# Register loads of a graph kernel's edge count: 32-bit places spread over partitions, or 16-bit places in one row; segment tables stored at once or in seven parts

## The chip, the cores and the metric

The kernel runs on one core of one Trainium2 chip. The metric is the time on the device in microseconds, the median of several executions. One further execution is recorded by the hardware profiler; all rows below come from it.

## What is computed

Four graph layers stand behind each other, each with a layer norm, a ReLU and a residual sum around it, over 3125 nodes of 128 features and one list of 103125 edges, sorted by destination.

```python
edge_index = jnp.stack([src, dst])
h = jnp.maximum(_layernorm(x, axis=-1), 0.0)
x = x + _L0_gnn_ref(h, edge_index, ...)      # segment_sum(x[src], dst) @ W_rel + b + x @ W_root, batch norm, relu
h = jnp.maximum(_layernorm(x, axis=-1), 0.0)
x = x + _L1_gnn_ref(h, ..., src, dst)        # two layers: mean over neighbours
h = jnp.maximum(_layernorm(x, axis=-1), 0.0)
x = x + _L2_gnn_ref(h, edge_index, ...)      # attention over edges, 8 heads
h = jnp.maximum(_layernorm(x, axis=-1), 0.0)
x = x + _L3_gnn_ref(h, ..., edge_index, edge_type_8)   # two layers, a weight matrix for each of 8 edge types
```

The first two layers need sums over neighbours only, so the kernel counts the edges between each pair of nodes once, in a table `adj` in DRAM, and multiplies by it.

## The kernel before, in words

**The stage of the change** builds `adj`. The edges lie in 806 tiles of 128. They are gone through in 84 epochs of 19 steps (`EPOCHS`, `STEPS_OF`). A step is one product on TensorE: a one-hot of the edges' source digit (128 columns) times a one-hot of 100 cells (`CELLS`), added into PSUM at a place that depends on the data. So each step has a place, a number up to 7600, that TensorE's instruction queue has to have in a register before it can issue the product. A twentieth place of each epoch (`SLOTS` is 20) says where the last block of the epoch before lies, which is carried over from SBUF by the product at L784.

The places are worked out on VectorE at lines 450 to 460 into `steprow`, a tile of 84 partitions (one for each epoch) with 32-bit integers; the last of these instructions gives the mark `stepped`. `places_of(e, lo, hi)` (L750) loads the places `lo` to `hi` of epoch `e` into TensorE's registers with one load instruction, from partition `e`. Four epochs are a window (`GROUP`), and `count_edges` spreads the loads over it: at the end of a window's fourth epoch it loads 20, 20 and the first 8 (`FEW`) places of the next three epochs; in the middle of the third epoch, before its step 8, the other 12; at that epoch's end the 20 of the fourth.

The other engines run beside this, each in a loop of its own. VectorE builds the one-hots of each epoch in two instructions (`compare_epochs`, L416 and L419), two epochs ahead at most, and in some epochs the moments of a tile of `X`. ScalarE (`move_out`, L809) copies each epoch's PSUM half into one of two windows in SBUF (`adj_window`, `chunk_and_window`), and from epoch 54 on does a tile of the first layer norm in each epoch; before that it waits for `s_seg`. SyncE's queue (`store_windows`, L831) stores a window of 3850 KB to `adj` when its four epochs are out, one store after the other; ScalarE may write a window again when its store has landed.

**The segment tables** (`relf`, `twice`, `seg`: for each tile of 128 edges where segments begin and end) are made on GpSimd at lines 716 to 727 and stored to `rel_tile` and `seg_tile` behind the fourth window's store (`w == 3`, L832 to L837). The attention layer reads them back some 1000 us later. They lie where ScalarE writes from epoch 54 on, hence its wait.

**The start.** SyncE's queue issues the inputs' transfers up to L376, then goes on to the windows' stores. `s_joint`, a trip of the step blocks through DRAM (L354 to L358), has the form of the trip that the change adds.

Of the kernel before, what the change touches and what calls it, by code (L numbers as in the profile page):

```python
# [4 lines left out]

F32 = mybir.dt.float32
I32 = mybir.dt.int32
F16 = mybir.dt.float16
B16 = mybir.dt.bfloat16
ALU = mybir.AluOpType  # L10
# [36 lines left out]
KT = 7  # L47
# [4 lines left out]
STEPS = EPOCHS * STEPS_OF  # L52
QUARTER = STEPS // 4
GROUP = 4
FEW = 8
WINDOWS = EPOCHS // GROUP
SPANNED = GROUP * STEPS_OF + 1
# [1 line left out]
CHUNKS = 7  # L59
DST = CHUNK * WD  # L60
BLOCKS = CHUNK * CHUNKS
assert (WINDOWS - 1) * GROUP * STEPS_OF - (ET - 1) >= CHUNK and RELU_FROM + NT <= EPOCHS
assert EPOCHS % GROUP == 0 and STEPS % 4 == 0 and STEPS >= ET + BLOCKS - 1 and KT * P >= BLOCKS
BEGUN = ((0, 4), (0, KT), (0, KT), (0, KT))
HELD = ((0, 4), (0, KT), (0, KT), (3, KT))
# [52 lines left out]
def build(nc, a, out):  # L118
    with ExitStack() as ctx:
# [69 lines left out]
        def dram(name, shape, dt=F32):  # L189
            return nc.dram_tensor(name, shape, dt, kind="Internal").ap()  # L190
# [2 lines left out]
        xs_t, xd_t = dram("xs_t", [NP, RW]), dram("xd_t", [W, RW])  # L193
        rel_t = [dram(f"rel_table{j}", [R * NP, P]) for j in (0, 1)]
        rel_tile = dram("rel_tile", [KT * P, P], F16)
        step_row = dram("step_row", [1, STEPS + 1 + EPOCHS], F16)
        seg_tile = dram("seg_tile", [KT * P, SEG])
        piece_t = dram("piece_t", [HEADS, PT * P // 2, 4])
# [21 lines left out]
        cells = tmp(dense, "edge_cell", [P, EPOCHS, SLOTS], F16)  # L220
        iota_lo = tmp(dense, "iota_lo", [P, P, STEPS_OF], F16)
        iota_cell = tmp(dense, "iota_cell", [P, CELLS, 2], F16)
        steprow = tmp(dense, "steprow", [EPOCHS, 32], I32)
        dstf = invdeg[:, 4 * P:(4 + KT) * P].rearrange("p (k e) -> p k e", e=P)
        relf = invdeg[:, (4 + KT) * P:(4 + 2 * KT) * P].bitcast(F16)[:, 0:KT * P].rearrange("p (k e) -> p k e", e=P)
        twice = invdeg[:, (4 + 2 * KT) * P:(4 + 3 * KT) * P].rearrange("p (k e) -> p k e", e=P)
        seg = H[:, :, :].rearrange("p t d -> p (t d)")[:, 0:KT * 3 * P].rearrange("p (k a e) -> p k a e", k=KT, a=3)
        epochrow = tmp(dense, "epochrow", [1, WINDOWS, 16], I32)
        windowrow = tmp(dense, "windowrow", [1, WINDOWS], I32)
        early = ExitStack()  # L230
# [194 lines left out]
        for j in range(4):  # L425
            T.need(found[j], centred)
            if j > 1:
                T.need(lod[j - 2], spread[j - 2])
            placed_d.append(look(4 + j, j, 1, 0))
            T.need(both, bsd[j])  # L430
            placed_c.append(look(j, j, 2, 1))
            T.need(within)
            if j > 1:
                T.need(celled[j - 2])
            looked = look((6, 7, 4, 5)[j], j, 0)
            A.need(placed_d[j])
            spread.append(A.did(nc.scalar.activation(far[:, quarter(j)], pb[4 + j][:, 0:QUARTER], ACT.Square,
                                                     bias=centre[:, 0:1])))
            A.need(looked)
            lod.append(A.did(nc.scalar.activation(los[:, 21 * j:21 * j + 21, :].rearrange("p e k -> p (e k)"),  # L440
                                                  pb[(6, 7, 4, 5)[j]][:, 0:QUARTER], ACT.Copy)))
            celled.append(cells_of_quarter(j))
            if j == 0:
                V.after(lod[0])
                compare_epoch(0)
            if j == 1:
                A.did(nc.scalar.activation(dstf[:, :, :], drow[:, :, :], ACT.Copy))
                copied = A.did(nc.scalar.activation(twice, twice.bitcast(I32), ACT.Copy))
                V.need(s_joint.now())
                V.did(nc.vector.tensor_scalar(jr[:, :], joint[:, 0:STEPS_OF], joint[:, 0:1], None, ALU.subtract))  # L450
                V.did(nc.vector.tensor_scalar(steprow[:, STEPS_OF:SLOTS], joint[:, 0:1], joint[:, STEPS_OF:SLOTS],
                                              float(CELLS), ALU.subtract, ALU.mult))
                V.did(V.after().tensor_scalar(turns[:, :], jr[:, :], float(SLOTS // 4), None, ALU.is_ge))
                for q in (2, 3):
                    V.did(V.after().scalar_tensor_tensor(out=turns[:, :], in0=jr[:, :], scalar=float(q * SLOTS // 4),
                                                         in1=turns[:, :], op0=ALU.is_ge, op1=ALU.add))
                V.did(V.after().tensor_scalar(jr[:, :], jr[:, :], float(CELLS), None, ALU.mult))
                stepped = V.did(V.after().scalar_tensor_tensor(
                    out=steprow[:, 0:STEPS_OF], in0=turns[:, :], scalar=float(512 - SLOTS // 4 * CELLS), in1=jr[:, :],
                    op0=ALU.mult, op1=ALU.add))  # L460
                b0w = b0[:, :].rearrange("p (w g) -> p w g", g=GROUP)
                V.did(nc.vector.tensor_scalar(b0[:, :], steps_of[:, :, 0], -1.0, float(CELLS), ALU.add, ALU.mult))
                V.did(V.after().tensor_copy(windowrow[:, :], b0w[:, :, 0]))
                windowed = V.did(V.after().tensor_tensor(epochrow[0:1, :, 0:GROUP], b0w,
                                                         b0w[:, :, 0:1].to_broadcast([1, WINDOWS, GROUP]), ALU.subtract))
        T.need(idn, s_raw.now(), lod[2])
        for j, n in enumerate(raw):
            tw = T.did(nc.tensor.transpose(pb[4][:, j * P:(j + 1) * P], wraw[n], ident[:, :]))
# [279 lines left out]
                    first_norm["shift"] = rows_shift(0, NT, (root_n, 1))  # L748

        def places_of(e, lo, hi):  # L750
            place = nc.values_load_multi_w_load_instructions(
                steprow[e:e + 1, lo:hi], engines=(ENG.PE,), min_val=0, max_val=(SPANNED - 1) * CELLS,
                skip_runtime_bounds_check_because="made on the chip from counts")[1]
            return [nc.s_assert_within(v, 0, 2048 - CELLS, skip_runtime_bounds_check_because="made on the chip")
                    for v in place[:STEPS_OF - lo]] + list(place[STEPS_OF - lo:])

        def count_edges():
            T.need(stepped)
            place = {0: places_of(0, 0, SLOTS)}
            T.need(celled[3], A.now())  # L760
            for e in range(EPOCHS):
                half = sums[:, (e % 2) * 2048:(e % 2 + 1) * 2048]
                if e > 1:
                    nc.tensor.wait_ge(eout_n, e - 1)
                for j in range(4):
                    nc.tensor.matmul(half[:, j * 512:j * 512 + SLOTS // 4 * CELLS], zeros[:, 0:P],  # L766
                                     zeros[:, 0:SLOTS // 4 * CELLS], start=True, stop=False)
                nc.tensor.wait_ge(ehot_n, e + 1)
                places = place.pop(e)
                for k in range(STEPS_OF):  # L770
                    if e % GROUP == 2 and k == FEW:
                        places = places + places_of(e, FEW, SLOTS)
                    m = nc.tensor.matmul(half[:, bass.ds(places[k], CELLS)], hot_lo[e % 2][:, :, k], hot_cell[e % 2][:, k // 2, :, k % 2],  # L773
                                         start=False, stop=False)
                m.then_inc(estep_n, 1)
                for j in range(1 if e else 0, 4):
                    m = nc.tensor.matmul(half[:, j * 512:j * 512 + 1], zeros[:, 0:P], zeros[:, 0:1], start=False, stop=True)
                if e == 0:
                    place.update({1: places_of(1, 0, SLOTS), 2: places_of(2, 0, FEW)})
                if e % GROUP == 2:  # L780
                    place[e + 1] = places_of(e + 1, 0, SLOTS)
                if e:
                    nc.tensor.wait_ge(eout_n, e)
                    m = nc.tensor.matmul(half[:, 0:CELLS], ident[:, :],  # L784
                                     filled[(e - 1) // GROUP % 2][:, bass.ds(places[STEPS_OF], CELLS)],
                                     start=False, stop=True)
                m.then_inc(ebuilt_n, 1)
                if e + 1 < EPOCHS and e % GROUP == GROUP - 1:
                    place.update((n, places_of(n, 0, SLOTS)) for n in (e + 1, e + 2))
                    place[e + 3] = places_of(e + 3, 0, FEW)  # L790
# [29 lines left out]
        def store_windows():  # L820
            nc.sync.wait_ge(*windowed)
            for w in range(WINDOWS):
# [8 lines left out]
                nc.sync.dma_start(adj[:, bass.ds(first, SPANNED * CELLS)], filled[w % 2][:, :]).then_inc(s_adj, 16)  # L831
                if w == 3:  # L832
                    nc.sync.wait_ge(*relled)
                    s_seg.did(nc.sync.dma_start(rel_tile.rearrange("(k p) e -> p k e", p=P), relf))
                    s_seg.did(nc.sync.dma_start(seg_tile[:, 3 * P:SEG].rearrange("(k p) s -> p k s", p=P), twice))
                    s_seg.did(nc.sync.dma_start(seg_tile[:, 0:3 * P].rearrange("(k p) s -> p k s", p=P),
                                                seg[:, :, :, :].rearrange("p k a e -> p k (a e)")))  # L837

        def load_chunk(c, b, *marks):
            for mark in marks:  # L840
# [960 lines left out]
```

## Time and profile before

| | |
|---|---|
| runs of the kernel | 4201.55, 4203.5, 4205.0 us; median 4203.5 |
| the profiled execution's own time | 4200.0 us |
| its span, first to last instruction | 4198.7 us |
| busy over the span | TensorE 72%, GpSimd 56%, VectorE 45%, ScalarE 17% |
| TensorE's mean granted clock | 0.702 of full speed |

The span is what the rows below count in, from 0; the time on the device is 1.3 us more. Busy shares are means over stages with different limits: the stage of the change lies in the first tenth of the span.

In the rows, PE is TensorE, PEld its weight loads, DVE VectorE, ACT ScalarE, POOL GpSimd, SP SyncE; a q behind the name is the engine's instruction queue. "x19" is a count. In brackets stands the idle time before, and what ended it; "issue" says that nothing in the profile did.

### The profile page before, as it was taken

The numbers are of one execution on the slowest core, as the hardware profiler recorded it, in microseconds if no ns is written. First come the engines' busy times: TensorE is split into PE (matmuls) and PEld (weight loads), VectorE is DVE, ScalarE is ACT, GpSimd is POOL, SyncE is SP. The second block draws the span as 40 slices with busy tenths as digits, with TensorE's granted clock in tenths as the row PEclk, the third lists the DMA queues.
The fourth block names the chain that finished last, engine by engine and source line by source line (L and its number), as shares of the span: only waits on it lengthen the run. The fifth ranks groups of instructions, "written<-read, shape, count | busy, mean of one in ns | idle before, by whom it ended". The sixth has DMA issues, their size and how long they took to land.

```text
span 4198.7 us, 42410 instructions
## 1 busy us (share of the span) xinstructions
PE 3033.3 (72%) x12147; PEld 1985.2 (47%) x12147; DVE 1903.7 (45%) x4160; ACT 713.2 (17%) x1945; POOL 2354.3 (56%) x2464
## 2 busy tenths in 40 slices
PE   6677889997888888887476666666677666666666
PEld 4555445554656656665243333333344333334334
DVE  6555675558889889897621111111122111111112
ACT  4344010002434434344300000000010000000000
POOL 3000000006777777775257777777775777777776
PEclk8777899998999989898665555555566555555555
DMA  4554745545444454553132222212233221211222
GB/s 178 209 217 199 321 192 225 216 167 132 118 112 116 114 111 119 111 119 83 42 126 53 53 52 53 53 52 53 53 100 112 53 53 52 53 53 53 53 53 64
DMA packets 237155, 456.14 MB, mean 109 GB/s; under 512 B 64259, under 2 KB 184001, under 8 KB 231816
## 3 DMA queue, kind: packets, MB, share of 16 engines
q1 hardware_dynamic: 159144, 291.46, 19.5%
q0 software_dynamic: 77792, 161.98, 15.6%
q8 instruction: 112, 1.84, 0.2%
q14 instruction: 107, 0.88, 0.1%
HBM read 336.69 MB, written 116.52 MB: 108 GB/s over the span
## 4 chain that ended last, share of the span: by engine, by line
PE 30%; DMA 27%; POOL 23%; issue 14%; DVE 4%; ACT 1%; SPq 0%; ACTq 0%; DVEq 0%; POOLq 0%
DMA edge_buffers<-rel_table,relidx 25%; POOL round_buffers L1209 15%; PE sums L872 9%; PE sums L661 8%; POOL edge_buffers L633 8%; PE sums L773 3%; PE sums L766 3%; PE sums L1699 2%; PE sums L784 1%; DMA adj<-adj_window 0%; DVE logits L1408 0%; PE sums L1253 0%; DMA adj_chunk<-adj 0%; DVE positive L1405 0%; PE sums L1331 0%
## 5 line engine op out<-in xcount | busy, mean ns | idle before, releaser
L633 POOL DMA_INDIRECT edge_buffers<-rel_table,relidx x1612 | 1529.5, 949 | 584.6 <-PE sums L661 415.1
L661 PE MATMUL sums<-edge_buffers 128*128 128x128 f32 x3224 | 1250.2, 494 | 748.7 <-DMA edge_buffers<-rel_table,relidx 744.8
L661 PEld LDWEIGHTS sums<-edge_buffers 128*128 128x128 f32 x3224 | 799.3, 309 | 1202.6 <-issue 1201.8
L1209 POOL DMA_INDIRECT round_buffers<-xs_t,srcs x806 | 763.7, 948 | 571.5 <-DMA xd_t<-round_buffers 326.1
L644 DVE TENSOR_SCALAR edge_buffers<-iota,rel 128x128 f32<-128x128 f32 x1612 | 334.4, 298 | 1639.2 <-PE sums L661 1639.2
L690 ACT ACTIVATE trio<-sums,c_L_b 128x256 f32<-128x256 f32 (+1 forms) x16 | 8.0, 500 | 2014.1 <-PE sums L665 2014.1
L1022 POOL IOTA trio<- 128x806 int32 x1 | 0.8, 805 | 566.1 <-ACT H L576 566.1
L1253 PE MATMUL sums<-round_buffers,ident 128*128 128x408 f32 x620 | 278.5, 533 | 25.8 <-DMA round_buffers<-xs_t,srcs 22.2
L1256 PEld LDWEIGHTS sums<-round_buffers 128*128 128x128 f32 x1612 | 244.1, 198 | 75.9 <-issue 65.2
L1353 ACT ACTIVATE trio<-sums 128x128 f32 x806 | 223.8, 278 | 279.1 <-PE sums L1331 205.5
L1331 PE MATMUL sums<-round_buffers 128*128 128x128 f32 x1612 | 243.0, 301 | 4.0 <-issue 2.0
L1256 PE MATMUL sums<-round_buffers 128*128 128x136 f32 x1612 | 245.6, 286 | 0.0
L872 PE MATMUL sums<-chunk_and_window,H 128*128 128x448 f32 x600 | 231.5, 546 | 7.3 <-issue 6.1
L1331 PEld LDWEIGHTS sums<-round_buffers 128*128 128x128 f32 x1612 | 218.5, 211 | 17.5 <-issue 14.4
L416 DVE TENSOR_TENSOR trio<-iota_lo,edge_lo 128x2432 f16<-128x2432 f16 x84 | 125.9, 1498 | 169.7 <-PE sums L773 168.8
L1405 DVE TENSOR_TENSOR positive<-positive,sums 128x384 f32<-128x384 f32 x310 | 152.9, 493 | 75.8 <-ACT positive L1343 75.5
L773 PEld LDWEIGHTS sums<-trio 128*128 128x128 f16 x1596 | 142.6, 152 | 75.5 <-issue 66.2
L773 PE MATMUL sums<-trio 128*128 128x100 f16 x1596 | 147.1, 257 | 42.7 <-issue 42.6
L872 PE MATMUL sums<-adj_chunk,H 128*128 128x448 f32 x450 | 173.6, 546 | 3.5 <-DMA adj_chunk<-adj 3.5
L872 PEld LDWEIGHTS sums<-chunk_and_window,H 128*128 128x128 f32 x600 | 115.2, 193 | 119.4 <-issue 117.7
L1394 DVE TENSOR_SCALAR round_buffers<-sums,pair_column 128x416 f32<-128x416 f32 x248 | 159.7, 644 | 12.0 <-PE sums L1271 11.2
L1408 DVE TENSOR_REDUCE logits<-positive 128x24 f32<-128x384 f32 x310 | 155.3, 501 | 10.7
(326 smaller groups left out, 2871.0 us busy)
## 6 DMA issues: line engine op xcount, KB each, us to landing
chunk_and_window<-adj SPq DMA_DIRECT2D x10, 5600.0 KB, 16.2
round_buffers<-xd_t SPq DMA_DIRECT2D x806, 68.0 KB
adj_chunk<-adj SPq DMA_DIRECT2D x9, 5600.0 KB, 16.0
adj<-adj_window SPq DMA_DIRECT2D x11, 3850.0 KB, 12.4
adj<-chunk_and_window SPq DMA_DIRECT2D x10, 3850.0 KB, 12.5
edge_buffers<-rel_table,relidx POOLq DMA_INDIRECT x1612, 2.5
rel_table<-table_stages SPq DMA_DIRECT2D x50, 512.0 KB, 2.6
round_buffers<-xs_t,srcs POOLq DMA_INDIRECT x806
```

The costliest lines, as they stand in the source:

```text
L633: nc.gpsimd.indirect_dma_start(slot(t), None, table[:, :], bass.IndirectOffsetOnAxis(ap=index[:, t:t + 1], axis=0)).then_inc(slot_sem(t), 16)
L644: made = nc.vector.tensor_scalar(round_hots(i)[:, k, :], iota[:, :], rel[:, t:t + 1], None, ALU.is_equal)
L661: nc.tensor.matmul(sums[:, bass.ds(place[k], P)], slot(t), round_hots(i)[:, k, :], start=False, stop=False).then_inc(summed_n, 1)
L773: m = nc.tensor.matmul(half[:, bass.ds(places[k], CELLS)], hot_lo[e % 2][:, :, k], hot_cell[e % 2][:, k // 2, :, k % 2], start=False, stop ...
L872: m = nc.tensor.matmul(ps.rearrange("p (b w) -> p b w", w=WD), tables[:, hi, :], held[b][:, :, hi, :], start=(hi == 0), stop=(hi == HI - 1))
L1209: nc.gpsimd.indirect_dma_start(rows[r % RING][:, k * RW:(k + 1) * RW], None, xs_t[:, :], bass.IndirectOffsetOnAxis(ap=srcs[:, t:t + 1], ax ...
L1253: nc.tensor.matmul(pb[2 + q % 2][:, 0:(hi - lo) * RW], ident[:, :], rows[r % RING][:, lo * RW:hi * RW], start=True, stop=False)
L1256: m = nc.tensor.matmul(pb[2 + q % 2][:, (k - lo) * RW:(k - lo + 1) * RW], hotT[r % 2][:, k * P:(k + 1) * P], win[r % 2][:, k * RW:(k + 1) ...
L1331: m = nc.tensor.matmul(pb[6 + q % 2][:, (k - lo) * P:(k - lo + 1) * P], msg[:, k * P:(k + 1) * P], hot[r % 2][:, k * P:(k + 1) * P], start ...
L1353: nc.scalar.activation(pairs[:, bass.ds(at[k], P)], pb[6 + q % 2][:, (k - lo) * P:(k - lo + 1) * P], ACT.Copy).then_inc(out_n, 1)
L1394: nc.vector.tensor_scalar(hotT[r % 2][:, j * QUART:(j + 1) * QUART], spread, paircol[:, 0:1], None, ALU.is_equal).then_inc(hotT_n, 1)
L1408: nc.vector.tensor_reduce(lgs[:, :].rearrange("p (h k) -> p k h", k=U)[:, lo:hi, :], lv.rearrange("p (k h c) -> p k h c", h=HEADS, c=HD), ...
```

## The change

The places are worked out as before, but written as 16-bit integers (`steprow` is now a 16-bit view of a tile of 32-bit words, 16 in each of 84 partitions). Two new transfers take the ten words of each epoch through DRAM (`reg_row`) into one row on partition 0, `regrow`, with 12 words for each epoch. Epoch 0 is still loaded from `steprow`; all others are loaded from `regrow`, as 16-bit numbers, after a wait for the second transfer (`T.need(regged)`, behind epoch 0's steps). How many registers a load fills, and when, is the same.

The three stores of the segment tables behind window 3 become three stores, of a seventh each, behind each of the windows 3 to 9.

```diff
+I16 = mybir.dt.int16
+WORDS = 12
...
+        reg_row = dram("reg_row", [EPOCHS, WORDS], I32)
...
-        steprow = tmp(dense, "steprow", [EPOCHS, 32], I32)
+        stepwords = tmp(dense, "step_words", [EPOCHS, 16], I32)
+        steprow = stepwords[:, :].bitcast(I16)
...
+        regrow = tmp(dense, "regrow", [1, EPOCHS * WORDS], I32)
...
+        s_regs = Dma(sem("s_register_row"))
+        nc.sync.wait_ge(*stepped)
+        regged = s_regs.did(nc.sync.dma_start(reg_row[:, 0:SLOTS // 2], stepwords[:, 0:SLOTS // 2]))
+        nc.sync.wait_ge(*regged)
+        regged = s_regs.did(nc.sync.dma_start(
+            regrow[:, :].rearrange("a (e k) -> a e k", k=WORDS)[:, :, 0:SLOTS // 2],
+            reg_row.rearrange("(a e) k -> a e k", a=1)[:, :, 0:SLOTS // 2]))
...
         def places_of(e, lo, hi):
+            row = regrow[:, :].bitcast(I16)[0:1, 2 * e * WORDS + lo:2 * e * WORDS + hi] if e else steprow[0:1, lo:hi]
             place = nc.values_load_multi_w_load_instructions(
-                steprow[e:e + 1, lo:hi], engines=(ENG.PE,), min_val=0, max_val=(SPANNED - 1) * CELLS,
+                row, engines=(ENG.PE,), min_val=0, max_val=(SPANNED - 1) * CELLS,
...
                 if e == 0:
+                    T.need(regged)
                     place.update({1: places_of(1, 0, SLOTS), 2: places_of(2, 0, FEW)})
...
                 if w == 3:
                     nc.sync.wait_ge(*relled)
-                    s_seg.did(nc.sync.dma_start(rel_tile.rearrange("(k p) e -> p k e", p=P), relf))
-                    s_seg.did(nc.sync.dma_start(seg_tile[:, 3 * P:SEG].rearrange("(k p) s -> p k s", p=P), twice))
-                    s_seg.did(nc.sync.dma_start(seg_tile[:, 0:3 * P].rearrange("(k p) s -> p k s", p=P),
-                                                seg[:, :, :, :].rearrange("p k a e -> p k (a e)")))
+                if 3 <= w < 3 + KT:
+                    rows = slice((w - 3) * P, (w - 2) * P)
+                    s_seg.did(nc.sync.dma_start(rel_tile[rows, :], relf[:, w - 3, :]))
+                    s_seg.did(nc.sync.dma_start(seg_tile[rows, 3 * P:SEG], twice[:, w - 3, :]))
+                    s_seg.did(nc.sync.dma_start(seg_tile[rows, 0:3 * P], seg[:, w - 3, :, :].rearrange("p a e -> p (a e)")))
```

## Rows read from the trace of the kernel before

**Rows 1.** Busy time by stretch: us, engines, TensorE clock, DMA share, GB/s
```profile
35.00:440.00 405.00, 287.12 (x2353) 216.17 (x2354) 225.16 (x200) 165.85 (x115) 33.59 (x12) 0.75 0.51 212
```

**Rows 2.** The chain that ended last, 35 to 440 us, by line
```profile
by line: PE sums L773 32.5%; PE sums L766 26.6%; issue 24.3%; PE sums L784 10.6%; DMA adj<-adj_window 4.9%; ACT adj_window L809 3.6%; PE sums L777 1.2%; ACT chunk_and_window L809 0.9%; ACTq L795 0.1%; ACTq L809 0.1%; ACT w_L_n L471 0.0%; AC
```

**Rows 3.** Timeline of TensorE, 384.5 to 402.5 us: start, us, what
```profile
393.13 1.48 PE L773 MATMUL sums<-trio 128*128 128x100 f16 x11 [2.16 <-issue]
...
402.19 0.58 PE L766 MATMUL sums<-zeros 128*128 128x500 f16 x2 [2.14 <-ACT adj_window L809]
```

**Rows 4.** Register loads of L751, one each: duration in ns, start in us
```profile
L751 PEldq TENSOR_LOAD <-steprow x1: 594/594/594, 39.6 to 39.6; - x1
...
L751 PEldq TENSOR_LOAD <-steprow x1: 849/849/849, 43.8 to 43.8; - x1
...
L751 PEldq TENSOR_LOAD <-steprow x1: 3464/3464/3464, 117.8 to 117.8; - x1
...
L751 PEldq TENSOR_LOAD <-steprow x1: 6004/6004/6004, 122.7 to 122.7; - x1
...
L751 PEldq TENSOR_LOAD <-steprow x1: 2647/2647/2647, 390.3 to 390.3; - x1
...
L751 PEldq TENSOR_LOAD <-steprow x1: 1379/1379/1379, 394.4 to 394.4; - x1
```

**Rows 5.** Timeline of SyncE's queue, 50 to 445 us
```profile
53.96 0.36 SPq L831 DMA_DIRECT2D adj<-adj_window  x1
...
111.65 0.33 SPq L831 DMA_DIRECT2D adj<-chunk_and_window  x1
...
113.69 8.77 SPq L836 DMA_DIRECT2D seg_tile<-H  x1
...
135.58 0.37 SPq L831 DMA_DIRECT2D adj<-adj_window  x1
...
384.38 0.33 SPq L831 DMA_DIRECT2D adj<-chunk_and_window  x1
...
402.16 0.33 SPq L831 DMA_DIRECT2D adj<-adj_window  x1
...
421.01 0.33 SPq L831 DMA_DIRECT2D adj<-chunk_and_window  x1
...
439.88 0.33 SPq L831 DMA_DIRECT2D adj<-adj_window  x1
```

**Rows 6.** Loads of 1, 4, 13, 3 and 8 registers at other lines: min/median/max ns
```profile
L823 SPq TENSOR_LOAD <-windowrow x21: 262/271/951, 34.4 to 421.4; - x21
...
L795 ACTq TENSOR_LOAD <-epochrow x21: 307/310/507, 34.8 to 419.0; - x21
...
L649 PEldq TENSOR_LOAD <-offrow x124: 1091/1102/2026, 2128.9 to 4174.1; - x124
...
L1599 PEldq TENSOR_LOAD <-pair_place x1: 964/964/964, 2010.2 to 2010.2; - x1
...
L1599 PEldq TENSOR_LOAD <-pair_place x1: 1942/1942/1942, 2024.8 to 2024.8; - x1
```

**Rows 7.** DMA busy in tenths, 40 slices of 384 to 404 us
```profile
DMA  0090910909091590919010100000001000000590
```

**Rows 8.** Groups of VectorE in that window: busy us, mean ns
```profile
L416 DVE TENSOR_TENSOR trio<-iota_lo,edge_lo 128x2432 f16<-128x2432 f16 x4 | 6.0, 1493 | 7.7 <-PE sums L773 7.6
...
L419 DVE TENSOR_TENSOR trio<-iota_cell,edge_cell 128x2000 f16<-128x2000 f16 x4 | 4.8, 1192 | 0.0
```

**Rows 9.** DMA issues, 20 to 45 us: KB each, us to landing
```profile
piece_dst<-in_piece_col SPq DMA_DIRECT2D x1, 6.5 KB, 8.1
```

**Rows 10.** Waits of SyncE's queue, 20 to 60 us
```profile
SPq L356 <- DMA step_row<-step_block: 0.9, 1, 0.9
```

**Rows 11.** Busy time by window of the stretch, columns as rows 1
```profile
384.40:402.20 17.80, 12.25 (x113) 9.61 (x111) 10.28 (x8) 8.89 (x9) 0.00 (x0) 0.90 0.53 223
402.20:421.00 18.80, 13.94 (x113) 10.57 (x114) 10.54 (x9) 8.68 (x8) 0.00 (x0) 0.70 0.49 211
```

More of the change, by code:

```diff
@@ L61 @@
 BLOCKS = CHUNK * CHUNKS
-assert (WINDOWS - 1) * GROUP * STEPS_OF - (ET - 1) >= CHUNK and RELU_FROM + NT <= EPOCHS
+assert (WINDOWS - 1) * GROUP * STEPS_OF - (ET - 1) >= CHUNK and GROUP * (4 + KT) <= RELU_FROM and RELU_FROM + NT <= EPOCHS
 assert EPOCHS % GROUP == 0 and STEPS % 4 == 0 and STEPS >= ET + BLOCKS - 1 and KT * P >= BLOCKS
```

## The prediction

> **What bounds the kernel now.** I first cut the span into stretches. The count of edges is the stretch from 35 to 440 us [rows 1]: 405 us, no engine over 75% busy, TensorE's mean granted clock 0.75, the DMA engines half used. So no engine's work is the bound as it stands. The chain of that stretch [rows 2] gives 24.3% to "issue", that is to TensorE waiting for nothing that the profile shows, no line of VectorE's among the first ten, and a few per cent to ScalarE. The timeline of TensorE in one window says where this lies [rows 3]: it stands idle 2.16 us before the last 11 steps of the window's third epoch and 2.14 us before the next window.
>
> The register loads of L751 fill just these holes [rows 4] (105 in all: one for each of 84 epochs, and a second in 21 of them). The one at 390.3 us takes 2.65 us and ends at 392.98; the steps go on at 393.13. A load stops TensorE's instruction queue. The reader is to see that the queue is the bound: from one store of a window to the next, 384.38 to 402.16, are 17.78 us [rows 5]; the loads in it are one of 12 registers (2.65), three of 20 (about 1.38 each) and one of 8 (about 0.60), 7.4 us in all, and 10.4 us are left for the instructions of four epochs, 2.6 us each. Over the stretch a window takes (439.88 - 53.96) / 20 = 19.3 us.
>
> What sets a load's price? A load that nothing disturbs costs 0.27 us for 1 register and 0.31 for 4 [rows 6], 0.59 for 8, 0.85 for 12, 1.38 for 20 [rows 4]; one of 13 takes 1.10 [rows 6]. So it is one read of 0.26 us for each four registers, 16 bytes, and one more for the thirteenth. Three registers cost 0.96, near three reads, and 8 that begin off a 16-byte boundary (place 3 of their row) cost 1.94, 0.24 for each register [rows 6]: what isn't a whole aligned piece seems to be read one by one.
>
> And what disturbs one: the same 12 registers cost 0.85 us at 43.8, before any store, and 2.65 at 390.3 or, the longest, 3.46 at 117.8 while a window is being stored [rows 4]. The DMA engines start eight rounds of packets from 385.0 to 393.0 us, 1.15 us apart, so they are full until some 394.3 [rows 7] (a slice shows packets where they begin). The load at 390.3 lies in that, the one at 394.4 just behind it. I take 2.8 us for the twenty such loads, nearer to the undisturbed window's, so a read takes about 0.93 us beside a store. The load of 20 at 122.7 lies in the segment tables' transfer and takes 6.00 us, and that window takes 135.58 - 111.65 = 23.9 us [rows 4, 5].
>
> **The change, part by part.**
>
> *Loads of 16-bit places.* The trace has no load of 16-bit numbers, so the price has to be bounded. Below: if a read brings 16 bytes whatever the type, 8 places come in one, and rows of 12 words (48 bytes) keep each epoch, and place 8 of it, aligned: 20 places (40 bytes) are 3 reads instead of 5, 12 are 2 instead of 3, 8 are 1 instead of 2. Above: every place by itself, as in the load off the boundary (0.24 us each), 4.9 us for 20. I take the lower, because every load on aligned data in this trace, on three engines, goes by 16 bytes; the row of 3 registers is what speaks against it.
>
> Per window then: the 12 go from 2.8 to 2 x 0.93 = 1.87 (-0.93). The next load, of 20, used to start 10.0 us after the store's issue (394.4 - 384.4), as the store's packets ran out. It now starts at +9.1, and one or two of its 3 reads meet the store: 0.93 + 0.27 + 0.27 = 1.5 to 0.93 + 0.93 + 0.27 = 2.1, where it cost 1.38; I take +0.3. The three behind the fourth epoch go from 1.38 + 1.38 + 0.60 to 0.85 + 0.85 + 0.31, -1.35. Sum -2.0 us; without the collision -2.8. Over 20 windows -40 us.
>
> Is something else late next? VectorE's comparison needs 1.49 + 1.19 = 2.7 us an epoch [rows 8], 10.7 in a window, plus 0.3 in the epochs with moments; a window of 17.3 us covers it. The store's 10 to 12 us fit too, though stores wait for each other. Neither binds.
>
> The Trainium skill, page "Runtime: NRT & Kernel Launch", section "Instruction fetch mechanics", gives a register load (it speaks of loads from HBM) about 200 ns for each register, in bulk too. By that 20 registers would cost 4.0 us; the trace has 1.38 [rows 4], 70 ns each, so the trace disagrees on the size. But the rule counts registers, not bytes, and by it a narrower type would save nothing in any load, and the sum would be the detour's 6 us alone.
>
> *The row's way through DRAM.* SyncE's queue issues two transfers that weren't there, with a wait between them, and TensorE waits for the second (`regged`) before it loads epoch 1. The wait for `stepped` is over when SyncE comes to it, behind the issue at 33.66. The transfer at 33.66 lands 8.1 us later, at 41.8 [rows 9], behind the index tables that are issued before it. The first new one is issued at about 34.4 and lands behind it, at 42; the second is issued then and takes 1 us (a like one, 3 KB, was waited for 0.9 us [rows 10]) to 3 us. So `regged` stands at 43.5 to 45.5, where TensorE was through with its loads at 40.2 (39.6 + 0.6 [rows 4]), the 1.4 us load of 20 before that one included. It now ends them at about 44.5 + 0.85 + 0.31 = 45.7: +5.5 us, once. Nothing hides it, as ScalarE and VectorE wait for TensorE's epoch 1. Behind it on SyncE stands only the first window's store, at 54. If the transfers overtook the queue it would be near 0; I keep 0 to +8.
>
> *Segment tables in seven parts.* Now three transfers (224 + 448 + 1344 KB) follow the fourth store, SyncE is held 8.77 us by the last [rows 5], and the 20-register load meets them. In parts, about 1 us of DMA stands behind each of seven stores. The load of 6.00 us falls back to about 1.5 (-4.5); in seven windows one read more of the load at +9.1 falls into the transfer, 0.65 us each (+4.5). I cost it at nothing, -5 to +5. ScalarE's wait for the tables at epoch 54 comes at about 36 + 54 x 4.8 = 295 us; the last part goes out behind the tenth store, by 36 + 10 x 19.3 = 229 us at the latest.
>
> **Sum.** -40 + 5.5 + 0 = -34.5 us. The profiled execution took 4200.0 (span 4198.7), so 4165.5; it lies 3.5 below the median of the runs shown, 4203.5, and on that scale I predict **4169 us**.
>
> **The rivals.** 0.2%, 8.4 us, is about what a measurement of this kernel can tell from no change.
>
> 1. *As above*, 4169, own range 4140 to 4190. Chance 0.54.
> 2. *A load costs by registers*, four to a read of whatever width. For it: all loads here are of 32-bit numbers, so the trace can't tell 16 bytes from four registers. Against it: 8 registers off a 16-byte boundary cost 1.94 [rows 6], so the address counts. The loads stay, the row's detour stays: +6, with the tables 0, so 4209. It is also the case in which the change does nothing for the loads. Chance 0.16. (The rule of the Trainium skill cited above, from "Runtime: NRT & Kernel Launch", points to this case.)
> 3. *The rest behind whole pieces is read singly.* 20 places are two pieces and four single ones, 6 reads; 12 are 5; 8 are 1. For it: 13 registers, and 3. The 12 beside the store: four reads of 0.93 and one free, 4.0 (+1.2); the 20 each 1.6 (+0.24, three times); 8 at 0.31 (-0.3). +1.6 a window, +32, with the detour +38: 4242. Chance 0.12.
> 4. *16-bit places are read one by one*, the other side of the bound. 12: five in the store and seven after, 6.3 us (+3.5); 20: 4.9 (+3.5, three times); 8: 1.9 (+1.3). +15.3 a window, 306 in all, 4203.5 + 306 + 6 = 4515. The forecast turns from gain to loss where 20 places cost more than about 1.3 us. Chance 0.10.
> 5. *More than forecast*: the load of 20 escapes the store (-2.8 a window, -57) and TensorE's clock falls less, since its idle times get shorter. The window from 402.2 had a mean of 0.70 of the clock and took 18.85 us (421.01 - 402.16), the one before it 0.90 and 17.78 [rows 5, 11]: 1 us a window, -20 at most. Against it: the stretch's mean is 0.75 [rows 1], and the idle times get shorter, but don't end. With the detour: -72, 4132. Chance 0.08.
>
> **The numbers.** Faster 0.54 + 0.08 = 0.62, same 0.16, slower 0.22. The range has to reach over rivals 2 and 3 and most of 5: 4130 to 4250; rival 4 lies outside.
>
> **What would show it.** The 20-register loads at about 0.85 us and those of 8 at 0.31 (rival 2: 1.38 and 0.60; 3: 1.6 and 0.31; 4: 4.9 and 1.9); the 12 beside a store near 1.9; the 20 loaded at the end of a window's third epoch longer than the others by 0.5 or more; stores of windows 17.3 us apart; epoch 1's loads beginning at 43 to 46 us; no load of 6 us, and no window of 24. The prediction is wrong first of all if the read isn't 16 bytes, then if something I called covered, a comparison or a store, takes up the holes that the loads leave.

## The result, and the profile after

The change made the kernel slower: 4577.01 us, the median of 4 runs (4568.01 to 4579.06), against 4204.25 (4201.55 to 4205.31) for the kernel before on the same chip. The ratio is 1.0882, with an interval of [1.0867, 1.0897]; that is +372.8 us. The forecast was -34.5. Ratios here leave out an execution that lies far above the others of its kernel; there was one, of 7972 us, among the ten of few12_seven below.

Where is the time? First the page's part 2 of the kernel after, its span in 40 slices of 114 us each:

```profile
span 4566.7 us, 42430 instructions
...
PE   4333333989978888888866666666667666666666
...
PEclk7666665989989999999987555555557555555555
```

The first seven slices, some 800 us, are a stage in which TensorE is busy a third of the time. Next the timeline of SyncE's queue, the stores of the first window, of two in the middle and of the last:

```profile
69.03 0.37 SPq L845 DMA_DIRECT2D adj<-adj_window  x1
...
445.83 0.34 SPq L845 DMA_DIRECT2D adj<-adj_window  x1
482.64 0.34 SPq L845 DMA_DIRECT2D adj<-chunk_and_window  x1
...
818.26 0.33 SPq L845 DMA_DIRECT2D adj<-adj_window  x1
```

A window takes (818.26 - 69.03) / 20 = 37.46 us, where it took 19.3 [rows 5]. The last store is issued 378.4 us later than before (439.88 [rows 5]); behind it the kernel is 10 us shorter than it was (4566.7 - 818.3 against 4198.7 - 439.9). So the whole loss lies in the count of edges. The chain from 35 to 820 us and the same window by itself:

```profile
by line: issue 56.6%; PE sums L786 16.6%; PE sums L779 14.5%; PE sums L798 5.5%; ACT adj_window L823 2.6%; ACT chunk_and_window L823 2.4%; DMA adj<-adj_window 1.4%; DMA reg_row<-step_words 0.9%; PE sums L790 0.6%; DMA regrow<-reg_row 0.3%; 
```
```profile
445.83:482.64 36.81, 14.22 (x112) 10.23 (x112) 10.64 (x10) 8.86 (x6) 0.00 (x0) 0.64 0.25 108
```

"issue" was 24.3% [rows 2]. The work in a window is what it was: 14.22 us of matmuls where two windows before had 12.25 and 13.94 [rows 11]. In the window's timeline of TensorE (start, us, what, and the idle time before it) the holes stand out:

```profile
460.01 1.82 PE L779 MATMUL sums<-zeros 128*128 128x500 f16 x4 [16.29 <-issue]
...
470.32 1.48 PE L786 MATMUL sums<-trio 128*128 128x100 f16 x11 [1.73 <-issue]
...
476.44 0.74 PE L798 MATMUL sums<-chunk_and_window,ident 128*128 x2 [4.58 <-issue]
```

The register loads, L764 in this kernel, one each, in ns, the last field the start in us; they answer to [rows 4]:

```profile
L764 PEldq TENSOR_LOAD <-regrow x1: 11262/11262/11262, 446.7 to 446.7; - x1
...
L764 PEldq TENSOR_LOAD <-regrow x1: 1916/1916/1916, 458.0 to 458.0; - x1
...
L764 PEldq TENSOR_LOAD <-regrow x1: 2852/2852/2852, 467.3 to 467.3; - x1
...
L764 PEldq TENSOR_LOAD <-regrow x1: 4720/4720/4720, 471.6 to 471.6; - x1
...
L764 PEldq TENSOR_LOAD <-regrow x1: 6031/6031/6031, 479.3 to 479.3; - x1
```

Undisturbed, 20 places now cost 4.72 us, 12 cost 2.85, 8 cost 1.92: each place 0.24 us, with no step at four or at eight. 20 places cost 1.38 before, and the same 12 cost 0.85 undisturbed. Where a load lies makes it worse. The window's store is issued at 445.83; the strip of the DMA engines (tenths, 40 slices of 440 to 500 us, 1.5 us each) shows it from 446 to 455 us, and the load of 20 at 446.7 lies in it and takes 11.26:

```profile
DMA  0000779779000000000000000000297797700000
```

Before, the load in the store was one of 12 registers and the three long ones lay outside. Now the first of the three loads at a window's end (at 479.3, behind the fourth epoch) takes 6.03 us, the store is issued meanwhile, the second load of 20 meets it, and the load of 12 at 467.3, 21 us behind the store's issue, is free of it.

All 105 loads together take 533.3 us in this trace and 163.9 in the one before, a difference of 369.4. That is nearly all of the 378.4 us by which the last store is later.

### The profile page after: what moved, and what is told of

The parts are those of the page before. It is cut to its first block, busy times and chain, and to the rows that moved or that the text cites. A ratio compares the mean times of both kernels' runs of the same rounds, so it can differ in the third digit from the quotient of the medians.

```text
span 4566.7 us, 42430 instructions
## 1 busy us (share of the span) xinstructions
PE 3038.7 (67%) x12147; PEld 1985.7 (43%) x12147; DVE 1902.3 (42%) x4160; ACT 712.9 (16%) x1945; POOL 2353.2 (52%) x2464
## 4 chain that ended last, share of the span: by engine, by line
PE 28%; DMA 24%; issue 20%; POOL 19%; DVE 7%; ACT 2%; SPq 0%; ACTq 0%; DVEq 0%; POOLq 0%
DMA edge_buffers<-rel_table,relidx 23%; POOL round_buffers L1224 11%; PE sums L887 8%; POOL edge_buffers L645 8%; PE sums L673 7%; PE sums L786 3%; PE sums L779 2%; PE sums L1714 2%; PE sums L798 1%; DVE logits L1423 1%; DVE positive L1420 1%; DVE round_buffers L1429 1%; DVE round_buffers L1409 1%; DVE round_buffers L1451 1%; PE sums L1268 1%
## 5 line engine op out<-in xcount | busy, mean ns | idle before, releaser
L779 PE MATMUL sums<-zeros 128*128 128x500 f16 x336 | 125.9, 516 | 346.9 <-issue 346.9
L779 PEld LDWEIGHTS sums<-zeros 128*128 128x128 f16 x336 | 42.2, 131 | 385.6 <-issue 377.7
L1409 DVE TENSOR_SCALAR round_buffers<-sums,pair_column 128x416 f32<-128x416 f32 x248 | 159.8, 644 | 11.2 <-PE sums L1286 9.9
```

Source lines behind the costliest of these rows:

```text
L1409: nc.vector.tensor_scalar(hotT[r % 2][:, j * QUART:(j + 1) * QUART], spread, paircol[:, 0:1], None, ALU.is_equal).then_inc(hotT_n, 1)
```

## The experiments

Ten kernels ran, in three groups, each on one chip beside the kernel before. On the chip of the first four the kernel before took 5164.9 us, on that of the last two 5062.7, on that of the other four 4203.4; what is longer on the first two lies behind the stage of the change, so ratios are taken on the same chip, and lengths of the stage are compared with [rows 5].

### The row alone, with 32-bit words (row32)

```diff
-WORDS = 12
+WORDS = 20
-        steprow = stepwords[:, :].bitcast(I16)
+        steprow = stepwords[:, :]
...
-            row = regrow[:, :].bitcast(I16)[0:1, 2 * e * WORDS + lo:2 * e * WORDS + hi] if e else steprow[0:1, lo:hi]
+            row = regrow[0:1, e * WORDS + lo:e * WORDS + hi] if e else steprow[0:1, lo:hi]
```

It is the kernel after, trip through DRAM and seven parts included, but with places of 32 bits.

> The changed kernel with everything kept (trip through DRAM, one row on partition 0, tables in seven parts) but the places as 32-bit words, 20 words for each epoch. Theory, the type does it: loads cost 1.38, 0.85 and 0.59 us again and only the later start of epoch 1 is left, 4204 + 6 = 4210 us. Rival, the row does it (a load from a row on partition 0 that a DMA wrote, or the wait): loads of 4.7 us remain, 4560 to 4580.

Measured: ratio 0.9991 [0.9976, 1.0006]. The loss is gone. Its register loads, of epochs 1 and 2, and of a window's 12 and 20:

```profile
L764 PEldq TENSOR_LOAD <-regrow x1: 1377/1377/1377, 44.1 to 44.1; - x1
...
L764 PEldq TENSOR_LOAD <-regrow x1: 596/596/596, 45.5 to 45.5; - x1
...
L764 PEldq TENSOR_LOAD <-regrow x1: 2644/2644/2644, 366.1 to 366.1; - x1
...
L764 PEldq TENSOR_LOAD <-regrow x1: 1359/1359/1359, 370.2 to 370.2; - x1
```

The prices are those of [rows 4]. So neither the row on partition 0 nor the trip costs anything in a load. The trip delays the first window's store by 4.9 us (58.89 against 53.96 [rows 5]), or by 6.2 against the kernel `seven` below, where it is issued at 52.70.

The ratio is under the forecast's 1.0014 all the same, and the traces point to a reason: from the row the loads are shorter. In the kernel before, an undisturbed load of 8 takes 0.587 us from partition 34 and 0.614 from partition 30, and the load of 12 beside a store takes 3.15 to 3.46 us from partitions 18 to 26 and 50 to 62, and 2.52 to 2.92 from the others. From partition 0, in row32, the same two take 0.586 to 0.596 and 2.34 to 2.99. Here is the load of 12 of epoch 50, before and in row32:

```profile
L751 PEldq TENSOR_LOAD <-steprow x1: 3324/3324/3324, 275.2 to 275.2; - x1
...
L764 PEldq TENSOR_LOAD <-regrow x1: 2637/2637/2637, 273.2 to 273.2; - x1
```

The loads of a window are 0.37 us shorter than in `seven`, some 7 us in all, about what the trip costs; the last store is issued at 435.21 here and at 435.80 there.

### 16 bits alone, without the row (part16)

```diff
-        steprow = tmp(dense, "steprow", [EPOCHS, 32], I32)
+        stepwords = tmp(dense, "step_words", [EPOCHS, 16], I32)
+        steprow = stepwords[:, :].bitcast(I16)
```

It is the kernel before with this edit only.

> The kernel before with 16-bit places, each epoch still in a partition of its own, loaded from there: no row, no trip, no wait, tables stored at once. Theory, the type does it: every place is a read of its own, 4.7 us for 20 where no store runs, 4577 less the later start (8 us), 4560 to 4575. Rival, the row: loads as before, 4200 to 4210.

Measured: ratio 1.0741 [1.0704, 1.0778], +385.6 us. All of its loads in one row (min/median/max), and one of 20 that lies in the segment tables' transfer, the table store at once being in this kernel:

```profile
L753 PEldq TENSOR_LOAD <-step_words x105: 1916/4739/16968, 31.9 to 815.2; - x105
...
L753 PEldq TENSOR_LOAD <-step_words x1: 16968/16968/16968, 179.8 to 179.8; - x1
```

The type alone brings the loss. It is 15 us more than the forecast's upper end. A window takes 38.06 us, where the kernel after needs 37.46: the load beside the table stores takes 17.0 us, 12.2 there, and an undisturbed one of 20 takes 4.72 to 4.99 us with the partition, always 4.72 there.

### The segment tables alone (seven)

```diff
-                if w == 3:
+                if 3 <= w < 3 + KT:
```

It is the kernel before with the stores in seven parts, as the change has them.

> The kernel before with the segment tables stored in seven parts alone. Both theories: no load of 6 us and no window of 24 us any more (-4.5), something back in seven windows; 4195 to 4207. If the parts were what costs, hundreds of us.

Measured: ratio 0.9986 [0.9971, 1.0002], 5157.54 us against 5164.9. The longest load of 20 takes 2.00 us, and the longest of all 3.43:

```profile
L751 PEldq TENSOR_LOAD <-steprow x105: 588/1390/3432, 31.9 to 427.9; - x105
```

The last store is issued at 435.80, 4.1 us earlier than [rows 5]; 1.3 of these it has at the first store already, before the edit acts. The interval takes in no change; the trace points to a gain of some 3 us, the medians to one of 7.

### 32 bits off the 16-byte boundary (shift32)

```diff
-        steprow = tmp(dense, "steprow", [EPOCHS, 32], I32)
+        steprow = tmp(dense, "steprow", [EPOCHS, 32], I32)[:, 1:32]
```

> The kernel before with the 32-bit places moved by one word in each partition, so that no load begins on a 16-byte boundary; nothing else. Theory, 32-bit words come four at a time only from a 16-byte boundary and singly otherwise, 0.24 us each as 16-bit places do: 4.8 us for 20, 4560 to 4580. Rival, the boundary has no part in it and what the later line (L1599) showed was disturbance: 4204.

Measured: ratio 1.0708 [1.0681, 1.0734], +366.7 us. Loads of 12, 20, 20, 20 and 8 registers in one window:

```profile
L751 PEldq TENSOR_LOAD <-steprow x1: 2869/2869/2869, 359.2 to 359.2; - x1
...
L751 PEldq TENSOR_LOAD <-steprow x1: 4732/4732/4732, 363.4 to 363.4; - x1
...
L751 PEldq TENSOR_LOAD <-steprow x1: 6039/6039/6039, 371.2 to 371.2; - x1
...
L751 PEldq TENSOR_LOAD <-steprow x1: 9913/9913/9913, 377.3 to 377.3; - x1
...
L751 PEldq TENSOR_LOAD <-steprow x1: 1936/1936/1936, 387.2 to 387.2; - x1
```

These are the loads of the kernel after, to 1% (2.85, 4.72, 6.03, 9.96, 1.92), with numbers twice as wide. For the two that meet a store this holds in this window; over the stage they vary, the one of 9.91 from 9.5 to 11.6 and once 17.0, beside the table stores. Whatever the load of 16-bit numbers does, it costs what a load does that can't take whole aligned pieces: one read for each register. ("Read" is a name for what these 0.24 us buy; the traces give durations only.)

### What the store does to a load (thin_store)

```diff
-                nc.sync.dma_start(adj[:, bass.ds(first, SPANNED * CELLS)], filled[w % 2][:, :]).then_inc(s_adj, 16)
+                nc.sync.dma_start(adj[:, bass.ds(first, SPANNED * CELLS // 7)], filled[w % 2][:, 0:SPANNED * CELLS // 7]).then_inc(s_adj, 16)
```

The kernel fills `adj` behind the last window (not shown) and reads its first chunk only after that.

> The kernel before, with each window's store cut to its first seventh (and the table filled afterwards from what lies in SBUF, so that it leaves out most of the edge counts); only the count stage's profile is read, the whole time holds some 13 full stores more. Theory: the register loads in the middle of a window are slow because a store of 3850 KB reads SBUF beside them. Then the loads of 12 fall from some 2.7 us to 0.85 like the undisturbed one, the loads of 20 lie at 1.36, and a window comes down from 19.2 to about 17.4 us, in the profile 345 us from the first store to the last in place of 386. Rival 1: the load waits for something of TensorE's own stream at that place; then the loads of 12 stay at 2.6 to 3.0 us and the window at 19.2. Rival 2: the loads get short but TensorE's products then bound the window, which stays above 18.5 us.

Measured: the load of 12 falls to 0.87 us, in all 21 windows to 0.85 to 1.28 (1.28 is the one in the segment tables' transfer), and the stores from 52.70 to 395.11 lie 17.12 us apart, 2.2 less than before. (The one execution, with the filling in it, took 4285.8 us.)

```profile
L751 PEldq TENSOR_LOAD <-steprow x1: 867/867/867, 368.6 to 368.6; - x1
```

The stores now land 2.7 to 4.4 us after their issue, in the kernel before, but for the last, after 10.8 to 12.9, and the load of 12 starts 6.5 to 8.6 us behind the issue, so it no longer has a store beside it. The store is what makes the load in the middle slow; both rivals fall.

### Fewer places beside the store (few12)

```diff
-FEW = 8
+FEW = 12
```

> The kernel before with the split of the third epoch's places moved: 12 places are loaded at the window's end and 8 in the middle of the third epoch (before: 8 and 12). Theory: an aligned load of 32-bit words costs one read for each four of them, some 0.26 us alone and 0.9 us beside a store. The load in the middle falls from 2.7 to 1.8 us, the one at the window's end rises from 0.59 to 0.85: -0.65 us a window, about -13 us in all, ratio 0.997. Rival: TensorE's products or the stores set the window, and its length stays within 0.1 us; the ratio is 1.000.

Measured: ratio 0.9974 [0.9965, 0.9984], 4193.06 us against 4203.44. The load of 8 in the middle, two reads beside the store, and the one of 12 at the window's end:

```profile
L751 PEldq TENSOR_LOAD <-steprow x1: 1743/1743/1743, 362.8 to 362.8; - x1
...
L751 PEldq TENSOR_LOAD <-steprow x1: 858/858/858, 372.6 to 372.6; - x1
```

The stores from 52.71 to 427.80 lie 18.75 us apart, 0.54 less (forecast 0.65). A read beside the store costs 0.87 us in this window, and 0.77 to 1.16 from the second window to the nineteenth (loads of 1.54 to 2.32 us); outside it costs 0.26 to 0.29.

### Two places in each 32-bit word (packed, packed4)

```diff
-                steprow[e:e + 1, lo:hi], engines=(ENG.PE,), min_val=0, max_val=(SPANNED - 1) * CELLS,
+                stepwords[e:e + 1, lo // 2:hi // 2], engines=(ENG.PE,), min_val=0, max_val=(SPANNED - 1) * CELLS * 65537,
...
+            place = [nc.s_assert_within(half, 0, (SPANNED - 1) * CELLS, skip_runtime_bounds_check_because="made on the chip")
+                     for word in words for half in (word & 65535, word >> 16)]
```

> The kernel before with two 16-bit places written in each 32-bit word of step_words, loaded as 32-bit words from the epoch's own partition, at 16-byte boundaries, and taken apart in registers: a load of 20 places fills 10 registers, of 12 places 6, of 8 places 4, and TensorE's queue gets some 10 register operations more an epoch. Theory (type and alignment decide): the words come four at a time and the two left over singly, so 10 words take 2 x 0.26 + 2 x 0.235 = about 1.05 us where 16-bit places took 4.72, 4 words take 0.31, and 6 words beside a store take 2.3 to 2.7. A window lies within 1 us of 19.2, and the time within 1% of that of the kernel before. Rival (16-bit data as such are slow, whoever reads them, because VectorE writes them so): 10 words take over 2 us and the ratio is above 1.02. What the register operations cost shows in the window: at 0.04 us each +1.5 us a window less some 1 us of shorter loads, +10 us in all; at 0.1 us each +4 us a window less 1, +60 us.

Measured: ratio 1.0081 [1.0066, 1.0097], +34.8 us. The loads of ten words, four and six:

```profile
L753 PEldq TENSOR_LOAD <-step_words x1: 1070/1070/1070, 371.8 to 371.8; - x1
...
L753 PEldq TENSOR_LOAD <-step_words x1: 336/336/336, 372.9 to 372.9; - x1
...
L753 PEldq TENSOR_LOAD <-step_words x1: 1052/1052/1052, 382.7 to 382.7; - x1
```

So the same 16-bit numbers, read as 32-bit words, cost 1.07 us for 20 places where the kernel after pays 4.72. The load of six words starts 9.4 us behind the store's issue, when little of the store is left, and so takes less than the 2.3 to 2.7 forecast. And yet a window is 20.94 us long, 1.6 more than before, where at most 1 was forecast. The next one takes the rest of the load away:

```diff
+                stepwords[e:e + 1, 0:12], engines=(ENG.PE,), min_val=0, max_val=(SPANNED - 1) * CELLS * 65537,
...
-                    if e % GROUP == 2 and k == FEW:
-                        places = places + places_of(e, FEW, SLOTS)
...
-                    place.update((n, places_of(n, 0, SLOTS)) for n in (e + 1, e + 2))
-                    place[e + 3] = places_of(e + 3, 0, FEW)
+                    place.update((n, places_of(n, 0, SLOTS)) for n in range(e + 1, e + 1 + GROUP))
```

> As with the packed words, and each epoch's 10 words are loaded as 12 (three whole pieces of four, the last two words zero), all four epochs of a window at its end; the load in the middle of the third epoch is gone. Theory (an aligned 32-bit load goes by pieces of four, and each waits in front of TensorE's queue): four loads of 0.85 us in a window, 3.4 us, where the kernel before has 7.5, less 1.5 us for 40 more register operations: -2.6 us a window, -55 us, ratio 0.987. The loads at the window's end lie close to the store of the window before; if the second to fourth still run beside one, each takes up to 2.6 us and the gain is gone (within 10 us of before). Rival: the register operations cost 0.1 us each; then the window is as long as before.

Measured: ratio 1.0026 [1.0016, 1.0035], +11.2 us; my forecast of -55 fell. The loads did what they should:

```profile
L754 PEldq TENSOR_LOAD <-step_words x76: 842/870/1642, 73.9 to 431.2; - x76
```

A window is 19.69 us all the same. Something else takes 4.4 us in it.

### The register operations by themselves (mask10)

```diff
+            place = [nc.s_assert_within(v & 8191, 0, (SPANNED - 1) * CELLS, skip_runtime_bounds_check_because="made on the chip")
+                     if k % 2 == 0 else v for k, v in enumerate(place)]
```

> The kernel before, whose loads stay as they are, with one register operation more (place AND 8191, which changes nothing) for every second place: 10 an epoch, 40 a window, as many as the packed kernels have. Theory (the register operations took what the packed words' shorter loads gave, some 4.3 us a window or 0.105 us each): the window rises from 19.3 to 23.5 us and the time by some 85 to 90 us, ratio 1.020 to 1.022. Rival (an operation costs some 0.04 us, and the packed kernels lost elsewhere, as by the wait from a packed load to its first product): +1.6 us a window, +34 us, ratio 1.008.

Measured: ratio 1.0049 [1.0032, 1.0066], +22.6 us, which is under both expectations; the stores from 57.12 to 470.33 lie 20.66 us apart, 1.36 more than before. Part of the price is hidden by a gain: the slower steps bring the load of 12 later behind the store, 9 to 10 us behind its issue in place of 6 to 7, and it takes 0.86 to 1.64 us outside the window with the segment tables. The table below takes the loads out: 40 register operations cost 14.51 - 11.55 = 2.96 us a window, 0.074 each, between the theory's 0.105 and the rival's 0.04. So they explain most of what the packed kernels lost, not all.

### The two gains together (few12_seven)

It is the kernel before with `FEW = 12` and the seven parts.

> The kernel before with 32-bit places, the segment tables in seven parts, and 12 of the third epoch's places loaded at the window's end, 8 in its middle. If the two gains add up (ratios 0.9974 for the split at 12 and 0.9986 for the parts alone, each by itself): 0.996, some 17 us faster than before, the last store issued at some 424 us in the profile. Rival: both take the same waiting away, and the ratio is that of the split alone, 0.997 to 0.998.

Measured: ratio 0.9964 [0.9943, 0.9985]; the medians are 5049.08 and 5062.69 us. The last store is issued at 425.34. It is faster than the kernel before, as forecast, but the interval doesn't tell it from few12 alone.

### One account for all of them

For each trace: the mean length of a window from the first store to the 21st (in thin_store the 21 short ones), the sum of the durations of TensorE's register loads between them divided by 20, and what is left.

| kernel | window, us | loads, us | rest, us |
|---|---|---|---|
| before | 19.30 | 7.74 | 11.55 |
| seven | 19.16 | 7.62 | 11.53 |
| row32 | 18.82 | 7.25 | 11.56 |
| few12 | 18.75 | 7.04 | 11.72 |
| few12_seven | 18.60 | 6.99 | 11.61 |
| thin_store | 17.12 | 5.54 | 11.58 |
| after | 37.46 | 25.46 | 12.01 |
| part16 | 38.06 | 26.03 | 12.03 |
| shift32 | 38.10 | 26.11 | 11.98 |
| mask10 | 20.66 | 6.15 | 14.51 |
| packed | 20.94 | 4.89 | 16.05 |
| packed4 | 19.69 | 3.71 | 15.98 |

With loads between 5.5 and 26.1 us a window, the rest stays between 11.5 and 12.0. A microsecond of register load is a microsecond of window, to some 3%: nothing covers it. The 0.45 us more where loads are long go with a lower clock (0.61 to 0.63 from the first store to the last in after, part16 and shift32, 0.74 in the kernel before); that it is the cause was not tried. The last three have 40 register operations more. In the packed ones another 1.5 us come on top; there the operation that puts a place into a product's address also takes the half out of the word (62 ns in the mean in place of 42, over some 370 of them from 250 to 350 us in both traces), 80 times 20 ns, 1.6 us. No run tries that by itself. The clock doesn't explain it: it is 0.74 in packed and 0.83 in packed4, with the same rest, and 0.79 in mask10.

## Why the prediction was wrong

**The step that failed** is "I take the lower, because every load on aligned data in this trace, on three engines, goes by 16 bytes". The premise was right and did not carry: all those loads were of 32-bit numbers. A load takes four registers in one read when they are 32-bit words at a 16-byte boundary, and one register in a read else: row32 against the kernel after, and part16 against the kernel before, change the type and nothing in a load's place; shift32 changes the address and nothing in the type, and gives the same prices. So the 12, the 20 and the 8 that the sum had at 1.87, 0.85 and 0.31 us took 2.85, 4.72 and 1.92 even undisturbed. The trace of before had the price of a single read in it, the 8 registers at 1.94 us [rows 6], and the upper bound was taken from it: 4.9 us for 20, measured 4.72. I gave that case 0.10 and left it out of the range. "The row of 3 registers" did point to single reads, but its 0.96 us [rows 6] is the price of four of them, not of three, as I read it; what the fourth is stays open. The error was in the choice between ends 4 us apart for a cost that occurs 105 times: no row was on the new type, and many rows on the old one don't make up for that.

The rule that I set against the sum, of the Trainium skill's page "Runtime: NRT & Kernel Launch", section "Instruction fetch mechanics", about 200 ns for each register in bulk, comes near it: 20 places in 16 bits take 4.72 us in the kernel after, 236 ns each, where an estimate by that rule gives 4.0. For aligned 32-bit words the measurement still goes against it, 69 ns each. And the time that I took from the rule, no saving and the detour's 6 us, was as wrong as the sum: by it the type changes nothing, and what the type changed is the loss.

**Rival 4 and what it lacked.** Its mechanism happened; its time, 4515, is 62 us short of 4577. It had the loads at 22.9 us a window (6.3 + 3 x 4.9 + 1.9), the trace has 25.5. The mechanism of the store was right, its place was not: I left the load of 12 in the store (6.3 us; it takes 2.85, 21 us behind the store's issue) and all of 20 outside it (one takes 10 to 12 us in each window). So -3.5 and about +6 a window. I moved the one load next to the edge by its own shortening and didn't lay out the window anew. The 0.45 us by which the rest of a window is longer are 9 us more.

**The trip through DRAM** was sized rightly. SyncE's queue and the first loads from the row:

```profile
33.66 0.66 SPq L473 DMA_DIRECT2D reg_row<-step_words  x1
40.56 0.92 SPq L475 DMA_DIRECT2D regrow<-reg_row  x1
```
```profile
L764 PEldq TENSOR_LOAD <-regrow x1: 4726/4726/4726, 43.0 to 43.0; - x1
```

The first transfer was issued 0.7 us before I had it and landed before 40.56, and TensorE's loads of epoch 1 begin at 43.0, just before the 43.5 to 45.5 forecast. In row32, where the loads are short, the loads of epochs 1 and 2 end at 45.5 + 0.6 = 46.1 (45.7 forecast), and the first store moves by 4.9 to 6.2 us (forecast +5.5). In whole times it can't be seen: row32, which has trip and seven parts, is at 0.9991, seven at 0.9986. The sum lacked the term that pays for it: loads from partition 0 are 0.37 us a window shorter.

**Seven parts**: costed at nothing, -5 to +5, and measured in seven at a gain of 3 us by the trace and 7 by the medians, neither clear of nothing. The load of 6.00 us [rows 4] went, as said. The price of one read more in seven windows showed in two of them, where a load of 20 takes 2.00 and 1.62 us in place of 1.36 and 1.38.

**The covers.** That VectorE and the stores don't bind held, in a harder form: the rest of a window is 11.5 to 12.0 us in all nine kernels without added register operations, though it held 5.5 to 26.1 us of loads.

**Bound of the stage.** "A load stops TensorE's instruction queue" and "the queue is the bound" held, and the size with them: 17.7 us of load more gave 18.2 us of window. The forecast had the right lever and pulled it the wrong way.

## What to carry to other kernels

Before a data type is narrowed for an instruction that reads it into registers, find one row of that type, or take the end of the bound that costs most: the price of a load goes by how many reads it is split into, and here only aligned 32-bit words came four at a time. Where a queue is the bound, put loads where no large transfer runs, and when their length changes, lay the whole window out again, since a load that gets longer moves into another transfer. Work taken out of a load and put into register operations on the same queue isn't saved: count the operations at their price in the queue, not at their duration.

## What the runs showed of the hardware that was not expected

- A load of 16-bit numbers costs what one of 32-bit numbers off a 16-byte boundary costs: 4.72 and 4.73 us for 20, 2.85 and 2.87 for 12, 1.92 and 1.94 for 8.
- Aligned 32-bit words: 0.34 us for 4 on TensorE, 0.59 for 8, 0.86 for 12, 1.36 for 20; 10 words 1.07, as two reads of four and two single ones.
- Beside a store of 3850 KB a read takes 0.77 to 1.16 us in place of 0.26 (few12: two reads 1.54 to 2.32); with the store landed, three take 0.87 (thin_store). The longest load, 20 places in part16, took 16.97 us beside a window's store and the segment tables.
- A load's price depends on the partition it reads, by some 5% undisturbed (8 registers 0.587 us from partition 34, 0.614 from 30) and by up to a quarter beside a store (12 registers 3.32 us from partition 50, 2.64 from partition 0 in row32).
- One register operation more on TensorE's queue is recorded with 32 ns and lengthens the window by 74 (mask10).
